# C in two buffers, GpSimd products two blocks wide, 28 weighed states, and the residual added by TensorE

## The chip, the cores and the metric

The kernel runs on one core of one Trainium2 chip. The metric is the device time of one execution in microseconds (us). The core has five engines that run their own instruction streams and meet only through semaphores: TensorE (PE in the profile, its weight loads PEld), VectorE (DVE), ScalarE (ACT), GpSimd (POOL) and SyncE (SP), which here only issues DMAs. SBUF is the on-chip memory, PSUM the memory that TensorE writes.

## The reference, cut to what matters

For 8 sequences of 1024 tokens, 512 features, the result is `x + mamba(layernorm(x)) + ffn(layernorm(x))`. The second term is the one that this change touches:

```python
xz = x @ W_in                       # 512 -> 2 * 1024
x_branch, z = split(xz)
xc = silu(causal_conv4(x_branch) + conv_b)
ssm = xc @ W_x                      # B (16), C (16) and one dt per token
dt = softplus(ssm[..., -1:] + dt_bias);  A = -exp(A_log)
for each token t:                   # h is [1024 channels, 16 states]
    h = h * exp(dt * A) + (dt * xc) * B
    y = sum over states of h * C
y = (y + xc * D_param) * silu(z)
out = x + y @ W_out + ffn
```

Everything is float32.

## The kernel before

The kernel has three phases. Phase W quantises the FFN's weights and phase A computes layer norm and FFN; it leaves `x + ffn` in the DRAM tensor `res_d`. Phase B computes the state-space term and adds it. Only phase B changes.

Phase B takes the 8192 tokens in 16 chunks of 512, two chunks to a sequence. The first chunk of a sequence (even) starts its scans at zero, the second (odd) at the states kept in `carry`. A chunk has 8 blocks of 128 channels, in two groups `g` of four, and 16 states. A slot `k` (0 to 31) is one state of one group; it has four steps, so that a step `n = 4k + j` runs from 0 to 127. In a step:

- ScalarE makes `decay = exp(dt * A)` (L1117) in one of three PSUM banks,
- GpSimd makes `v = u * B` (L963, function `drive`), with `u = dt * xc` and B of the state repeated over the partitions in `b_rep`; `v` has two buffers, one state each, and `v` of slot k may be written only when the scans of slot k-2 have read theirs,
- VectorE scans along the tokens, `hs = decay * hs + v` (L1159, `scan`), 128 channels by 512 tokens,
- TensorE turns one token tile of the previous state to tokens by channels (L1288, `ht`, two PSUM banks), and VectorE adds it to the sum, `acc = ht * C + acc` (L1173, `add_state`), C being one number per token from `c_now`.

For 20 of the 32 slots (the table `WEIGHED`) the last of the four token tiles takes another way: GpSimd multiplies the states by C (L971, `weigh`, output `hw`), TensorE turns and sums them in the PSUM bank `yw` (L1298), and VectorE adds that bank to `acc` once per group (L1181, `add_weighed`). So a chunk has 128 scans and 128 - 20 = 108 adds. GpSimd writes `hw` of slot k-2 right after the four `v` of slot k, and VectorE may not start the scans of slot k before `hw` of slot k-2 has been read out of the state buffer.

Between these steps stands the rest of the chunk's work, by tables of step or slot numbers: `MM` for TensorE (projections `ip` and `z`, convolution `cv`, `ssm`, turns `xd`, `yt`, and the output product `wo`, all through the two PSUM banks `mm`), `ACT_AT` for ScalarE (copies out of those banks, silu with its table loads, the parts of softplus), `POOL_AT` for GpSimd (`sp`: last add of softplus, `du`: `u = dt * xc`, `y2`: `acc * silu(z)`), `DVE_AT` for VectorE and `SP_AT` for SyncE. An engine waits at each such instruction for what it needs, and everything behind it on that engine waits too. ScalarE runs about two steps ahead of VectorE (three decay banks).

The output product `wo` of a token tile is four matmuls. After it VectorE adds the residual rows, `rtb = mm + rtb` (L1144), where SyncE has loaded `rtb` from `res_d` (`load`), and SyncE stores the sum (`store`). C of a chunk is copied by ScalarE from TensorE's bank to `c_next` (L1052) and by VectorE at step 4 to `c_now` (L1198), once the chunk before has used its own.

Of the kernel before, what the change touches and what calls it, by code (L numbers as in the profile page):

```python
# [16 lines left out]
ALU = mybir.AluOpType  # L17
ACT = mybir.ActivationFunctionType
# [618 lines left out]
def phase_b(nc, ctx, xnt, res, ssm_d, tap_d, ident, out, W_in, conv_w, conv_b, W_x, A_log, D_param, dt_bias, W_out):  # L637
# [27 lines left out]
    WEIGHED = (2, 3, 4, 6, 8, 10, 12, 13, 14, 15, 16, 17, 18, 19, 22, 23, 24, 25, 26, 30)  # L665
# [33 lines left out]
    c_now, c_next = sb("c_now", [P, NT, NS]), sb("c_next", [P, NT, NS])  # L699
# [17 lines left out]
    ct_done, ct_copied, c_set = sem("ct_done"), sem("ct_copied"), sem("c_set")  # L717
# [290 lines left out]
    def _(act):  # L1008
# [4 lines left out]
        def extra(c, what, *args):  # L1013
# [30 lines left out]
            if what in ("ssm", "ct"):  # L1044
# [86 lines left out]
    def _(dve):  # L1131
# [7 lines left out]
        def extra(c, what, g, t):  # L1139
            o = whose(c, what, g)  # L1140
            if o.exists(NC):
                wait(dve, rt_loaded[t % 2], o.at(64, 32 * g + 16 * (t // 2) + 16))
                wait(dve, wo_done, o.at(8, 4 * g + t + 1))
# [19 lines left out]
        def add_state(c, n):  # L1163

            g, s, k, t = n // 64, n // 4 % NS, n // 4, n % 4
            if s == 0 or (t == LT and all((NS * g + i, t) not in add_no for i in range(s))):
                wait(dve, acc_set, c.at(8, 4 * g + 4))
                if g == 0 and t == 0:
                    wait(dve, c_set, c.at(1, 1))
            else:  # L1170
# [3 lines left out]
                                           scalar=c_now[:, t, s:s + 1], in1=acc[g][:, t, :],  # L1174
# [9 lines left out]
        def part(c):  # L1184
            for n in range(4 * SLOTS):
# [174 lines left out]
```

## Time and profile before

| what | value |
|---|---|
| median of 3 runs | 5687.29 us (5685.86 to 5698.21) |
| the profiled execution | 5686.64 us, span 5684.8 us |
| busy share of the span | PE 86%, DVE 86%, POOL 70%, ACT 50% |
| phase B, first scan to last | 1935 to 5660 us |
| landing of one load of `rtb` | 4.2 us (median) |

Busy time is time in which an engine executes at least one instruction. One instruction's duration overlaps with the next one's by some tens of nanoseconds, so what an instruction costs its engine is read from start to start. The slices of the page before 1900 us are phases W and A, where TensorE is the busiest; from there on VectorE is at 9 tenths or more in each of them.

### The profile page before, as it was taken

The numbers are of one execution on the slowest core, as the hardware profiler recorded it, in microseconds if no ns is written. First come the engines' busy times: TensorE is split into PE (matmuls) and PEld (weight loads), VectorE is DVE, ScalarE is ACT, GpSimd is POOL, SyncE is SP. The second block draws the span as 40 slices with busy tenths as digits, with TensorE's granted clock in tenths as the row PEclk, the third lists the DMA queues.
The fourth block names the chain that finished last, engine by engine and source line by source line (L and its number), as shares of the span: only waits on it lengthen the run. The fifth ranks groups of instructions, "written<-read, shape, count | busy, mean of one in ns | idle before, by whom it ended". The sixth has DMA issues, their size and how long they took to land.

```text
span 5684.8 us, 79958 instructions
## 1 busy us (share of the span) xinstructions
PE 4886.1 (86%) x21764; PEld 3186.2 (56%) x21764; DVE 4871.6 (86%) x6055; ACT 2821.3 (50%) x4591; POOL 3984.9 (70%) x3130
## 2 busy tenths in 40 slices
PE   1799999999998788888888888888888888888867
PEld 1588888888886344444444444444444444444444
DVE  6676676676674399999999999999999999999998
ACT  1111111111111576666666666666667666667654
POOL 4333333333332499899999889989999998989996
PEclk9999999999999899999999999999999999999978
DMA  2111111111112222222232222322223232322221
GB/s 76 32 43 41 41 44 41 41 44 41 41 43 66 65 87 87 92 85 91 83 104 82 87 86 81 109 77 90 86 88 103 78 94 84 99 86 85 80 79 61
DMA packets 273645, 415.04 MB, mean 73 GB/s; under 512 B 31824, under 2 KB 105552, under 8 KB 269152
## 3 DMA queue, kind: packets, MB, share of 16 engines
q1 hardware_dynamic: 273248, 410.62, 22.8%
q8 instruction: 142, 2.33, 0.2%
q14 instruction: 255, 2.09, 0.1%
HBM read 340.23 MB, written 70.29 MB: 72 GB/s over the span
## 4 chain that ended last, share of the span: by engine, by line
DVE 23%; issue 18%; POOL 11%; PE 7%; ACT 7%; DVEq 1%; DMA 0%; POOLq 0%; ACTq 0%; SPq 0%
DVE hs L1159 14%; POOL v L963 8%; DVE acc L1173 8%; ACT decay L1117 3%; PE mm L1275 2%; PE ht L1288 2%; PE mm L1227 1%; DVEq L823 1%; POOL dt L989 1%; POOL sz L985 1%; ACT L1042 1%; POOL hw L971 1%; ACT xc L1042 1%; DVE rtb L1144 1%; PE mm L1244 1%
## 5 line engine op out<-in xcount | busy, mean ns | idle before, releaser
L963 POOL TENSOR_TENSOR v<-u,b_rep 128x512 f32<-128x512 f32 x2048 | 2555.2, 1274 | 201.9 <-DVE hs L1159 188.0
L1117 ACT ACTIVATE decay<-dt,a_neg 128x512 f32<-128x512 f32 x2048 | 1399.5, 688 | 1061.0 <-DVE hs L1159 1033.6
L1288 PEld LDWEIGHTS ht<-ident,hs 128*128 128x128 f32 x6912 | 827.8, 146 | 1503.4 <-issue 629.3
L1288 PE MATMUL ht<-ident,hs 128*128 128x128 f32 x6912 | 1127.5, 288 | 500.8 <-DVE acc L1173 318.6
L1159 DVE TENSOR_TENSOR_SCAN hs<-decay,v 128x512 f32<-128x512 f32 x1024 | 1232.3, 1216 | 152.3 <-POOL v L963 108.4
L1159 DVE TENSOR_TENSOR_SCAN hs<-decay,carry,v 128x512 f32<-128x512 f32 x1024 | 1293.3, 1275 | 26.7 <-ACT decay L1117 17.5
L1173 DVE SCALAR_TENSOR_TENSOR acc<-ht,c_now,acc 128x512 f32<-128x512 f32 x1728 | 1262.1, 730 | 11.9 <-PE ht L1288 11.4
L490 ACT ACTIVATE sg<-gate 128x512 f32<-128x512 f32 (+1 forms) x192 | 108.0, 563 | 1331.7 <-PE up L536 1331.7
L1275 PE MATMUL mm<-w_out,yt 128*128 128x512 f32 x1024 | 517.2, 612 | 43.5 <-ACT xb L1027 26.4
L1227 PE MATMUL mm<-x_in,w_in 128*128 128x512 f32 x1024 | 534.6, 634 | 21.3 <-DMA x_in<-xnt_d 17.8
L1244 PE MATMUL mm<-w_in,x_z 128*128 128x512 f32 x1024 | 507.0, 603 | 0.0
L1236 PE MATMUL mm<-xb,tap_diag 128*128 128x512 f32 (+3 forms) x1024 | 498.9, 599 | 2.7 <-ACT xc L1037 1.9
L106 POOL TENSOR_TENSOR h<-h,h_small 128x1408 f32<-128x1408 f32 x64 | 166.2, 2597 | 440.1 <-DVE h_small L100 440.1
L971 POOL TENSOR_TENSOR hw<-hs,c_rep 128x512 f32<-128x512 f32 x320 | 407.7, 1274 | 6.2 <-DVE hs L1159 6.2
L151 POOL TENSOR_TENSOR h<-h,h_small 128x1408 f32<-128x1408 f32 x64 | 166.3, 2598 | 333.7 <-DVE h L145 333.7
L435 DVE TENSOR_TENSOR rt<-down,rt 128x512 f32<-128x512 f32 x64 | 44.3, 692 | 322.2 <-PE down L536 322.2
L534 PE MATMUL gate<-gu,xqt 128*128 128x512 f32 (+1 forms) x768 | 300.7, 391 | 5.4 <-DVE xqt L426 5.4
L535 PE MATMUL gate<-gu,xqt 128*128 128x512 f32 (+1 forms) x768 | 288.8, 376 | 0.0
L536 PE MATMUL gate<-gu,xqt 128*128 128x512 f32 (+1 forms) x768 | 288.7, 376 | 0.0
L535 PE MATMUL up<-gu,xqt 128*128 128x512 f32 (+1 forms) x768 | 288.5, 376 | 0.0
L534 PE MATMUL up<-gu,xqt 128*128 128x512 f32 (+1 forms) x768 | 288.5, 376 | 0.0
L536 PE MATMUL up<-gu,xqt 128*128 128x512 f32 (+1 forms) x768 | 288.5, 376 | 0.0
(126 smaller groups left out, 7655.0 us busy)
## 6 DMA issues: line engine op xcount, KB each, us to landing
b_rep<-ssm_d SPq DMA_DIRECT2D x512, 256.0 KB, 3.4
tap_diag<-tap_d SPq DMA_DIRECT2D x128, 256.0 KB, 3.3
w_out<-in_L_attn_W_out SPq DMA_DIRECT2D x32, 1024.0 KB, 6.9
rtb<-res_d SPq DMA_DIRECT2D x128, 256.0 KB, 4.2
c_rep<-ssm_d SPq DMA_DIRECT2D x320, 64.0 KB, 3.2
xt<-in_L_attn_x SPq DMA_DIRECT2D x64, 256.0 KB, 2.8
xnt_d<-xntb SPq DMA_DIRECT2D x64, 256.0 KB, 2.7
rt<-in_L_attn_x SPq DMA_DIRECT2D x64, 256.0 KB, 2.6
```

The costliest lines, as they stand in the source:

```text
L534: nc.tensor.matmul(out, left_hi, right_hi, start=(k == 0), stop=False)
L535: nc.tensor.matmul(out, left_hi, right_lo, start=False, stop=False)
L536: last = nc.tensor.matmul(out, left_lo, right_hi, start=False, stop=(k == len(pairs) - 1))
L963: nc.gpsimd.tensor_tensor(v[k % 2][:, j, :], u[g][:, j, :], b_rep[k % 4][:, :], ALU.mult).then_inc(v_ready, 1)
L1117: nc.scalar.activation(decay[n % 3][:, :], dt[g][:, j, :], ACT.Exp, scale=a_neg[:, GD * g + j, s:s + 1]).then_inc(decay_ready, 1)
L1159: nc.vector.tensor_tensor_scan(h[k % 2][:, j, :], decay[n % 3][:, :], v[k % 2][:, j, :], carry[:, s, GD * g + j:GD * g + j + 1] if c.secon ...
L1173: nc.vector.scalar_tensor_tensor(out=acc[g][:, t, :], in0=ht[add_no[k, t] % 2][:, :, :].rearrange("p j d -> p (j d)"), scalar=c_now[:, t, ...
L1227: made, done = nc.tensor.matmul(bank[:, :], w_in[:, k, i * P:(i + 1) * P], x_in[:, k, :], start=first, stop=last), ip_done
L1236: made, done = nc.tensor.matmul(bank[:, skip:], tap_diag[i % 2][:, tap, :], xb[i % 2][:, tap + skip:tap + CL], start=first, stop=last), cv ...
L1244: made, done = nc.tensor.matmul(bank[:, :], x_z[:, k, t * P:(t + 1) * P], w_in[:, k, DI + g * GW:DI + (g + 1) * GW], start=first, stop=las ...
L1275: made, done = nc.tensor.matmul(bank[:, :], yt[t % 2][:, j, :], w_out[:, j, :], start=first, stop=last), wo_done
L1288: last = nc.tensor.transpose(ht[add_no[k, t] % 2][:, j, :], h[k % 2][:, j, t * P:(t + 1) * P], ident[:, :])
```

## The change

1. `c_now` becomes two buffers by chunk parity. ScalarE copies C straight into the one of its chunk, and VectorE's copy is gone, with `c_next` and the semaphore `c_set`.
2. `drive`, `sp`, `du` and `y2` work on two blocks per instruction (128 x 1024), B being repeated over the two by its access pattern. `POOL_AT` has 12 instructions in 12 entries where it had 24, and they stand at other slots: `y2` of group 1 at slots 3 and 4, `sp` and `du` at 7, 11, 29 and 31.
3. `WEIGHED` has 28 slots where it had 20: added are 0, 1, 7, 11, 20, 21, 28 and 31. Left out are 5, 9, 27 and 29.
4. `wo` has a fifth matmul, identity times the residual rows `rtb`, which waits for their load. ScalarE copies the bank into `rtb` (`add` in `ACT_AT`); `DVE_AT` is gone.
5. `ACT_AT` is written anew with these copies, 3 steps after the product's last matmul; silu of blocks 2 and 3 moves from step 38 to 47.

```diff
-    WEIGHED = (2, 3, 4, 6, 8, 10, 12, 13, 14, 15, 16, 17, 18, 19, 22, 23, 24, 25, 26, 30)
+    WEIGHED = (0, 1, 2, 3, 4, 6, 7, 8, 10, 11, 12, 13, 14, 15, 16, 17, 18, 19, 20, 21, 22, 23, 24, 25, 26, 28, 30, 31)
-    c_now, c_next = sb("c_now", [P, NT, NS]), sb("c_next", [P, NT, NS])
+    c_now = [sb(f"c_now{p}", [P, NT, NS]) for p in range(2)]
-    UNITS = {"ip": KH, "cv": KC, "z": KH, "wo": GD, "ssm": ND, "xd": 1, "yt": 1, "ct": 1}
+    UNITS = {"ip": KH, "cv": KC, "z": KH, "wo": GD + 1, "ssm": ND, "xd": 1, "yt": 1, "ct": 1}
...
             g = k // NS
-            for j in range(GD):
+            for j in range(0, GD, 2):
                 if j == 0:
                     wait(pool, b_loaded[k % 4], c.at(128, 16 * (k // 4) + 16))
                 if k % NS == 0:
-                    wait(pool, u_ready, c.at(8, 4 * g + j + 1))
-                wait(pool, scanned, c.at(128, 4 * (k - 2) + j + 1))
-                nc.gpsimd.tensor_tensor(v[k % 2][:, j, :], u[g][:, j, :], b_rep[k % 4][:, :], ALU.mult).then_inc(v_ready, 1)
+                    wait(pool, u_ready, c.at(8, 4 * g + j + 2))
+                wait(pool, scanned, c.at(128, 4 * (k - 2) + j + 2))
+                nc.gpsimd.tensor_tensor(v[k % 2][:, j:j + 2, :], u[g][:, j:j + 2, :],
+                                        b_rep[k % 4][:, :].unsqueeze(1).broadcast_to([P, 2, CL]),
+                                        ALU.mult).then_inc(v_ready, 2)
...
-                    wait(act, c_set, o.at(1, 0))
+                    wait(act, summed, o.at(ADDS, -ADDS))
                     wait(act, ct_done, o.at(1, 1))
-                    nc.scalar.activation(c_next[:, :, :], mm[bank_of("ct")][:, 0:NT * NS].rearrange("p (t s) -> p t s", t=NT),
+                    nc.scalar.activation(c_now[o.r % 2][:, :, :], mm[bank_of("ct")][:, 0:NT * NS].rearrange("p (t s) -> p t s", t=NT),
...
+            elif what == "add":
+                wait(act, wo_done, o.at(8, 4 * g + t + 1))
+                nc.scalar.activation(rt[t % 2][:, :], mm[bank_of("wo", g, t)][:, :], ACT.Copy).then_inc(added, 1)
...
-                nc.vector.tensor_tensor(rt[t % 2][:, :], mm[bank_of("wo", g, t)][:, :], rt[t % 2][:, :],
-                                        ALU.add).then_inc(added, 1)
...
-                if n == LAG - 1 and c.exists(NC):
-                    wait(dve, summed, c.at(ADDS, 0))
-                    wait(dve, ct_copied, c.at(1, 1))
-                    nc.vector.tensor_copy(c_now[:, :, :], c_next[:, :, :]).then_inc(c_set, 1)
...
-                made, done = nc.tensor.matmul(bank[:, :], yt[t % 2][:, j, :], w_out[:, j, :],
-                                              start=first, stop=last), wo_done
+                if last:
+                    wait(pe, rt_loaded[t % 2], o.at(64, 32 * g + 16 * (t // 2) + 16))
+                left, right = (ident[:, :], rt[t % 2][:, :]) if last else (yt[t % 2][:, j, :], w_out[:, j, :])
+                made, done = nc.tensor.matmul(bank[:, :], left, right, start=first, stop=last), wo_done
```

GpSimd, slots 1 to 5 of an odd chunk (v: products of one state, hw: weighed state, sz: `y2`). Before:

```order
L963 TENSOR_TENSOR v<-u,b_rep 128x512 x8
L985 TENSOR_TENSOR sz<-acc,sz 128x512 x2
L963 TENSOR_TENSOR v<-u,b_rep 128x512 x4
L985 TENSOR_TENSOR sz<-acc,sz 128x512 x2
L963 TENSOR_TENSOR v<-u,b_rep 128x512 x4
L971 TENSOR_TENSOR hw<-hs,c_rep 128x512
L963 TENSOR_TENSOR v<-u,b_rep 128x512 x4
```

Slots 3 to 5 of that chunk in the changed kernel:

```order
L960 TENSOR_TENSOR v<-u,b_rep 128x1024 x2
L970 TENSOR_TENSOR hw<-hs,c_rep 128x512
L985 TENSOR_TENSOR sz<-acc,sz 128x1024
L960 TENSOR_TENSOR v<-u,b_rep 128x1024 x2
L970 TENSOR_TENSOR hw<-hs,c_rep 128x512
L985 TENSOR_TENSOR sz<-acc,sz 128x1024
L960 TENSOR_TENSOR v<-u,b_rep 128x1024 x2
L970 TENSOR_TENSOR hw<-hs,c_rep 128x512
```

Each pair of narrow instructions is one wide one, a weighed product now stands in each of these slots, and one `y2` stands in each of two slots.

VectorE at the start of an odd chunk (hs: scan, acc: add), where the copy of C stood at step 4. Before:

```order
L1173 SCALAR_TENSOR_TENSOR acc<-ht,c_now,acc 128x512
L1159 SCALAR_TENSOR_TENSOR hs<-decay,carry,v 128x512
L1173 SCALAR_TENSOR_TENSOR acc<-ht,c_now,acc 128x512
L1198 COPY c_now<-c_next 128x64
L1159 SCALAR_TENSOR_TENSOR hs<-decay,carry,v 128x512
```

In the changed kernel, the first slots of that chunk:

```order
L1155 SCALAR_TENSOR_TENSOR hs<-decay,carry,v 128x512
L1169 SCALAR_TENSOR_TENSOR acc<-ht,c_now,acc 128x512
L1155 SCALAR_TENSOR_TENSOR hs<-decay,carry,v 128x512 x2
L1169 SCALAR_TENSOR_TENSOR acc<-ht,c_now,acc 128x512
L1155 SCALAR_TENSOR_TENSOR hs<-decay,carry,v 128x512
```

The copy is gone, and two scans stand together once per slot, where the fourth add was.

TensorE at the end of one output product of group 0 (mm: the shared banks). Before:

```order
L1275 MATMUL mm<-w_out,yt 128x512 x2
L1288 MATMUL ht<-ident,hs 128x128 x4
L1275 MATMUL mm<-w_out,yt 128x512
L1288 MATMUL ht<-ident,hs 128x128 x4
L1256 MATMUL mm<-ident,ssm_sb 128x16 x4
```

In the changed kernel:

```order
L1268 MATMUL mm<-w_out,yt 128x512 x2
L1280 MATMUL ht<-ident,hs 128x128 x4
L1290 MATMUL yw<-ident,hw 128x128 x4
L1268 MATMUL mm<-w_out,yt 128x512
L1280 MATMUL ht<-ident,hs 128x128 x4
L1268 MATMUL mm<-rtb,ident 128x512
L1246 MATMUL mm<-ident,ssm_sb 128x16 x4
```

The residual rows enter as a fifth product of the same size, one step later.

## Rows read from the trace of the kernel before

**Rows 1.** Windows of 233 us over phase B: time of the window, busy us (instructions) by engine.

```profile
sum 3726.00, PE 3143.45 PEld 1752.41 DVE 3622.32 ACT 2475.82 POOL 3388.55; mean PE 196.47 PEld 109.53 DVE 226.40 ACT 154.74 POOL 211.78
```

**Rows 2.** VectorE's groups in phase B: busy us, mean ns | idle before, releaser.

```profile
L1159 DVE TENSOR_TENSOR_SCAN hs<-decay,carry,v 128x512 f32<-128x512 f32 x1024 | 1293.3, 1275 | 26.7 <-ACT decay L1117 17.5 <-PE ht L1288 9.1
L1173 DVE SCALAR_TENSOR_TENSOR acc<-ht,c_now,acc 128x512 f32<-128x512 f32 x1728 | 1262.1, 730 | 11.9 <-PE ht L1288 11.4
L1159 DVE TENSOR_TENSOR_SCAN hs<-decay,v 128x512 f32<-128x512 f32 x1020 | 1227.4, 1216 | 45.4 <-ACT decay L1117 26.2 <-PE ht L1288 9.6 <-POOL hw L971 5.8
L1144 DVE TENSOR_TENSOR rtb<-mm,rtb 128x512 f32<-128x512 f32 x124 | 84.8, 684 | 17.0 <-PE mm L1275 16.8
L1198 DVE COPY c_now<-c_next 128x64 f32<-128x64 f32 x16 | 39.9, 2494 | 1.6
```

**Rows 3.** VectorE's waits in phase B: us in total, times, longest.

```profile
DVE hs L1159 <- ACT decay L1117: 43.7, 39, 1.8
DVE hs L1159 <- PE ht L1288: 18.7, 17, 1.6
DVE rtb L1144 <- PE mm L1275: 16.8, 19, 2.3
DVE hs L1159 <- POOL hw L971: 5.8, 4, 1.9
```

**Rows 4.** GpSimd's groups in phase B.

```profile
L963 POOL TENSOR_TENSOR v<-u,b_rep 128x512 f32<-128x512 f32 x2043 | 2549.1, 1274 | 201.9 <-DVE hs L1159 188.0 <-issue 12.6
L971 POOL TENSOR_TENSOR hw<-hs,c_rep 128x512 f32<-128x512 f32 x320 | 407.7, 1274 | 6.2 <-DVE hs L1159 6.2
L985 POOL TENSOR_TENSOR sz<-acc,sz 128x512 f32<-128x512 f32 x128 | 160.7, 1272 | 111.6 <-DVE acc L1173 41.9 <-DVE acc L1181 35.5 <-ACT sz L1059 34.1
L989 POOL TENSOR_TENSOR dt<-dt,u 128x512 f32<-128x512 f32 x124 | 157.9, 1273 | 0.0
```

**Rows 5.** Timeline of VectorE around one residual add: start, duration.

```profile
3507.89 0.73 DVE L1173 SCALAR_TENSOR_TENSOR acc<-ht,c_now,acc 128x512 f32<-128x512 f32 x1
3508.53 0.69 DVE L1144 TENSOR_TENSOR rtb<-mm,rtb 128x512 f32<-128x512 f32 x1
3509.13 2.33 DVE L1159 TENSOR_TENSOR_SCAN hs<-decay,v 128x512 f32<-128x512 f32 x2
3511.38 0.73 DVE L1173 SCALAR_TENSOR_TENSOR acc<-ht,c_now,acc 128x512 f32<-128x512 f32 x1
```

**Rows 6.** Timeline at two copies of C, the first with GpSimd at rest.

```profile
1941.50 0.17 DVE L1198 COPY c_now<-c_next 128x64 f32<-128x64 f32 x1
...
2867.29 1.27 POOL L985 TENSOR_TENSOR sz<-acc,sz 128x512 f32<-128x512 f32 x1
2867.48 2.37 DVE L1198 COPY c_now<-c_next 128x64 f32<-128x64 f32 x1
...
2869.76 1.21 DVE L1159 TENSOR_TENSOR_SCAN hs<-decay,v 128x512 f32<-128x512 f32 x1
```

**Rows 7.** GpSimd's groups by form, phase A: one operation at two widths.

```profile
L151 POOL TENSOR_TENSOR h<-h,h_small 128x1408 f32<-128x1408 f32 x64 | 166.3, 2598 | 333.7 <-DVE h L145 333.7
...
L151 POOL TENSOR_TENSOR xq<-xq,q_small 128x512 f32<-128x512 f32 x64 | 68.0, 1063 | 195.7 <-DVE xq L145 195.7
```

**Rows 8.** Timeline of GpSimd at slots 21 to 23 of an even chunk.

```profile
3004.37 3.82 POOL L963 TENSOR_TENSOR v<-u,b_rep 128x512 f32<-128x512 f32 x3
...
3014.25 2.50 POOL L985 TENSOR_TENSOR sz<-acc,sz 128x512 f32<-128x512 f32 x2 [4.29 <-ACT sz L1059]
3016.71 4.95 POOL L963 TENSOR_TENSOR v<-u,b_rep 128x512 f32<-128x512 f32 x4
```

**Rows 9.** The nearest forms to the new copy and the new product.

```profile
L1037 ACT ACTIVATE xc<-mm 128x512 f32<-128x512 f32 x128 | 75.2, 588 | 47.9 <-PE mm L1236 47.2
...
3001.87 1.88 PE L1244 MATMUL mm<-w_in,x_z 128*128 128x512 f32 x4
```

**Rows 10.** Timeline of the loads of residual rows behind a store.

```profile
3509.86 0.33 SPq L930 DMA_DIRECT2D rtb<-res_d  x1
...
3516.69 0.67 DVE L1144 TENSOR_TENSOR rtb<-mm,rtb 128x512 f32<-128x512 f32 x1
```

More of the change, by code:

```diff
@@ L771, in phase_b @@
-    DVE_AT = {21: [("add", 1, 0)], 29: [("add", 1, 1)], 42: [("add", 1, 2)], 50: [("add", 1, 3)],
-              94: [("add", 0, 0)], 99: [("add", 0, 1)], 104: [("add", 0, 2)], 109: [("add", 0, 3)]}
-    POOL_AT = {2: [("y2", 1, 0), ("y2", 1, 1)], 3: [("y2", 1, 2), ("y2", 1, 3)], 7: [("sp", 1, 0), ("du", 1, 0)],
[3 rows of a table removed]
+    ACT_AT = {4: [("silu_z", 1, 0), ("silu_z", 1, 1)], 6: [("ip", 0), ("abs", 1, 0)], 7: [("abs", 1, 1)],
+              8: [("abs", 1, 2)], 9: [("ip", 1), ("abs", 1, 3)], 10: [("exp", 1, 0)],
+              12: [("cv", 0), ("relu", 1, 0)], 13: [("yt", 1, 0), ("relu", 1, 1), ("exp", 1, 1)],
+              16: [("ip", 2), ("relu", 1, 2), ("relu", 1, 3)], 19: [("cv", 1)], 20: [("yt", 1, 1)],
+              21: [("ln", 1, 0), ("ln", 1, 1)], 23: [("add", 1, 0)], 26: [("ip", 3)], 28: [("xs", 1, 0)],
+              29: [("cv", 2)], 30: [("xs", 1, 1)], 31: [("silu_xc", 0), ("silu_xc", 1)], 33: [("add", 1, 1)],
+              34: [("yt", 1, 2)], 37: [("cv", 3)], 38: [("xd", 1, 0)], 39: [("xs", 1, 2)],
+              41: [("ip", 4), ("yt", 1, 3)], 42: [("xs", 1, 3)], 45: [("add", 1, 2)], 46: [("xd", 1, 1)],
+              47: [("silu_xc", 2), ("silu_xc", 3)], 49: [("ip", 5)], 53: [("xd", 1, 2), ("add", 1, 3)],
[3 rows of a table added]
+              87: [("z", 0, 3), ("silu_z", 0, 0), ("silu_z", 0, 1)], 92: [("ssm",), ("yt", 0, 0)],
+              93: [("yt", 0, 1)], 96: [("xs", 0, 0)], 97: [("abs", 0, 0), ("add", 0, 0)],
+              98: [("ct",), ("xs", 0, 1), ("abs", 0, 1)], 99: [("abs", 0, 2)], 100: [("abs", 0, 3)],
+              101: [("add", 0, 1)], 102: [("yt", 0, 2), ("exp", 0, 0)], 103: [("xd", 0, 0), ("exp", 0, 1)],
[4 rows of a table added]
@@ L973, in weigh, with extra @@
                                     ALU.mult).then_inc(weighed, 1)
-        def extra(c, what, g, j):
+        def extra(c, what, g, half):
             o = whose(c, what, g)
@@ L978, in extra @@
                 return
+            j = 2 * half
+            two = slice(j, j + 2)
             if what == "y2":
-                wait(pool, z_ready, o.at(4, 2 * g + j // 2 + 1))
-                if j == LT:
+                wait(pool, z_ready, o.at(4, 2 * g + half + 1))
+                wait(pool, summed, sums(o, NS * g + NS - 1, j + 1))
+                if half == LT // 2:
                     wait(pool, yw_added, o.at(2, g + 1))
-                else:
-                    wait(pool, summed, sums(o, NS * g + NS - 1, j))
-                nc.gpsimd.tensor_tensor(sz[:, j, :], acc[g][:, j, :], sz[:, j, :], ALU.mult).then_inc(y2_ready, 1)
+                nc.gpsimd.tensor_tensor(sz[:, two, :], acc[g][:, two, :], sz[:, two, :], ALU.mult).then_inc(y2_ready, 2)
             elif what == "sp":
-                wait(pool, sp_ops, o.at(16, 8 * g + 7 + j // 2))
-                wait(pool, relu_set, o.at(8, 4 * g + j + 1))
-                nc.gpsimd.tensor_tensor(dt[g][:, j, :], dt[g][:, j, :], u[g][:, j, :], ALU.add).then_inc(dt_ready, 1)
-            else:
-                wait(pool, xc_ready, o.at(ND, GD * g + j + 1))
-                wait(pool, dt_ready, o.at(8, 4 * g + j + 1))
-                nc.gpsimd.tensor_tensor(u[g][:, j, :], dt[g][:, j, :], xc[:, GD * g + j, :], ALU.mult).then_inc(u_ready, 1)
+                wait(pool, sp_ops, o.at(16, 8 * g + 7 + half))
+                wait(pool, relu_set, o.at(8, 4 * g + j + 2))
+                nc.gpsimd.tensor_tensor(dt[g][:, two, :], dt[g][:, two, :], u[g][:, two, :], ALU.add).then_inc(dt_ready, 2)
+            else:
+                wait(pool, xc_ready, o.at(ND, GD * g + j + 2))
+                wait(pool, dt_ready, o.at(8, 4 * g + j + 2))
+                nc.gpsimd.tensor_tensor(u[g][:, two, :], dt[g][:, two, :], xc[:, GD * g + j:GD * g + j + 2, :],
+                                        ALU.mult).then_inc(u_ready, 2)
         def part(c):
@@ L1137, in _ @@
             nc.vector.tensor_copy(w_x[:, :, a:a + n], w_x_raw[:, :, b:b + n]).then_inc(w_set, 1)
[L1139 to L1143, printed above, removed]
-                nc.vector.tensor_tensor(rt[t % 2][:, :], mm[bank_of("wo", g, t)][:, :], rt[t % 2][:, :],
-                                        ALU.add).then_inc(added, 1)
         def scan(c, n):
@@ L1168, in add_state @@
                 if g == 0 and t == 0:
-                    wait(dve, c_set, c.at(1, 1))
+                    wait(dve, ct_copied, c.at(1, 1))
             else:
@@ L1194, in part @@
                         add_weighed(owner, g)
-                if n == LAG - 1 and c.exists(NC):
-                    wait(dve, summed, c.at(ADDS, 0))
-                    wait(dve, ct_copied, c.at(1, 1))
-                    nc.vector.tensor_copy(c_now[:, :, :], c_next[:, :, :]).then_inc(c_set, 1)
-                for what in DVE_AT.get(n, ()):
-                    extra(c, *what)
         over_chunks(dve, part)
```

17 lines of the change are left out of this document (5 added, 12 removed), and 18 rows, old and new, of tables (ACT_AT, POOL_AT).

## The prediction

> **What bounds the kernel now.** I read the busy shares by stage first. Over phase B all engines stand in one row [rows 1]: of a window of 233 us VectorE is busy 226.4, GpSimd 211.8, TensorE 196.5, ScalarE 154.7. The 3726 us are 16 chunks of 232.9 us. VectorE's groups and waits come next [rows 2, 3]: it idles only 104 us in 3726, chiefly for decays (43.7), turned states (18.7), the output product (16.8) and weighed states (5.8). So VectorE's own work sets the time and its removal shortens the chunk one for one, until something else is late. GpSimd is the one to watch, 14.6 us a chunk behind. Its idle time is mostly waiting for VectorE [rows 4]: 188.0 us for scans that free `v`.
>
> What an instruction costs VectorE is its start-to-start time [rows 5]: an add 0.64 us (3507.89 to 3508.53), a residual add 0.60, a scan 1.125 (two in 2.25); in odd chunks the scan's mean is 0.059 us longer [rows 2], so 1.185. For GpSimd four `v` end 4.95 us after the first starts [rows 8], which with 1.274 for the last [rows 4] is (4.95 - 1.27) / 3 = 1.23 a step. Check: 128 `v`, 20 `hw` and 24 others make 172 x 1.23 = 211.6 us, as measured.
>
> **The change, VectorE's side.**
> - Eight more weighed slots remove 8 adds a chunk: 128 x 0.64 = 82 us. The add of `yw` stays, one a group.
> - The residual adds: 124 in phase B's windows x 0.60 = 74 us, and 17 us of waiting before them [rows 2] = 91 us.
> - The copy of C: 64 elements take 0.17 us with GpSimd at rest and 2.37 us beside it, ending only when the running GpSimd product has ended [rows 6]; the next scan starts 2.28 us after it started. 39.9 us in all, less 16 overlaps of 0.1: 38 us.
>
> The trace thus shows the copy held up for the length of GpSimd instructions. The Trainium skill (SBUF — State Buffer, "SBUF: two separate sides") calls the port pair of the two engines an exclusive lock held for the full instruction, for a VectorE operation in a 2-port mode or with two SBUF inputs. By it a copy left in place would now wait for instructions twice as long, some 38 us more; that is an estimate for a copy that is gone and so changes no sum.
>
> Together 82 + 91 + 38 = 211 us, 13.2 a chunk. VectorE's busy time falls from 226.4 to 226.4 - (211 - 17) / 16 = 214.3 us.
>
> A rule against moving the eight adds to GpSimd: the skill (Perfetto Trace Analysis, "Optimizing Scalar/DVE Operations") says that the two share an SBUF read port, so offloading between them might not help. Here the trace disagrees for these forms: 226.4 and 211.8 us busy in the same 233 [rows 1] must overlap by 205, with scans and adds at their usual step. Scans and adds read one operand from PSUM.
>
> **GpSimd's side.** A 128x1024 product doesn't stand in the trace. Bounds: twice a narrow one, 2.46 us a step; or less by the part that doesn't grow with width. Two widths of one operation give it [rows 7]: (2598 - 1063) / 896 = 1.713 ns an element, which leaves 1063 - 512 x 1.713 = 186 ns. Then a wide product lasts 2 x 1.274 - 0.186 = 2.36 us, a step of 2.32 after 0.045 of overlap. I take 2.32, since the form is the same but for what it reads; repeating an operand costs nothing in `hw`, which repeats C and takes the same 1274 ns [rows 4]. In a sentence that the sum does without: the skill (GPSIMD Engine Reference, "Elementwise — side-by-side cycle accounting") has 4497 ns for 2048 elements, and a line from there to 1274 at 512 estimates 2.35 at 1024.
>
> Per chunk: 64 + 12 = 76 wide x 2.32 = 176.3, 28 `hw` x 1.23 = 34.4, together 210.7. The 8 new `hw` (9.8) are paid by the 76 pairs (10.6). GpSimd is as busy as before in a chunk that VectorE could do in about 220: still second, but the room is small, and it is had only where the order allows.
>
> The order: `hw` of slot k-2 comes behind both `v` of slot k, and the scans of slot k wait for it. From the end of scans k-2, GpSimd needs 2.32 + 1.23 = 3.55 us, while VectorE has one slot, 4 x 1.125 + 3 x 0.64 = 6.42 us: 2.9 us of room. A slot costs GpSimd 5.87, so it gains 0.55 (0.79 in odd chunks) a slot. Where `sp` and `du` stand, two wide ones, 4.64 us go in at once; those slots (7, 11, 29, 31) have no `hw` due, so room is two slots: 2.32 + 4.64 + 4.64 + 1.23 = 12.83 against 12.84. One alone fits; the next ones come before it is made good. Walking even chunks so gives stalls of 1.1 at slot 0 (29 and 31 together), 1.5 at 5 (`y2` at 3 and 4), 1.2 at 8, 0.5 at 12, and 2.5 at 23 and 24, where the first `y2` still waits for silu (4.29 us) [rows 8] before `v` of 23 can follow: 6.8 us. Odd chunks, with 0.24 us more a slot, about 4. VectorE is idle anyway at some of these places (behind silu's table loads and at chunk starts), which takes about 2 off. I take 3.5 us a chunk, 56 in all; bounds 0 (all hidden) and 6.8 x 16 = 109.
>
> **The rest.** ScalarE gets 8 copies like that of `xc`, 0.59 each [rows 9], 4.7 us a chunk on an engine that has 78 free; they stand where decays are two steps ahead. TensorE gets 8 products; four take 1.88 us, 0.43 to 0.47 each [rows 9], 3.8 us a chunk beside 36 free. Their cover is the two `ht` banks. Cost 0; if a copy or product delays every fifth decay or turn, up to 0.5 each, 8 x 0.5 x 16 = 64 us. The new wait on TensorE is for the residual load, and all turns stand behind it. The tightest is tile 2 of group 0: loaded at 3509.86 behind the store, landing 4.2 us later at 3514.1, used at 3516.69 [rows 10]: 2.6 us spare, and the product uses it about as early as the add did. Cost 0 to 2 us a chunk; I take 0. SyncE's stores come when ScalarE's copy does, which runs ahead of VectorE, so its queue isn't later.
>
> Edges: before the first scan and behind the last one nothing is hidden. Wider pieces delay the first `v` and the first `y2` by about 1.1 us each (2.36 against 1.27), each waits for one more piece of input (1 to 2 us), and the last products add about 1: 6 us.
>
> **Sum.** 211 - 56 - 6 = 149 us less than the profiled execution's 5686.6 (0.7 under the median of the runs): 5537 us, a chunk of about 223.5.
>
> **The rivals.**
> - Nothing new is late: GpSimd's stalls all fall into idle time that exists. For it: its idle total stays above 8 us a chunk. Against: the walk above. 5686.6 - 211 + 6, about 5480.
> - GpSimd becomes the bound, the wide product saving nothing. 76 x 2.46 + 34.4 = 221.4, plus waits that no order removes, those for silu and the `yw` sum, (34.1 + 35.5) / 16 = 4.3 [rows 4], some of them shorter: 226.5 a chunk; (232.9 - 226.5) x 16 = 102, less 6: 5591. For it: the operation of rows 7 repeats one operand within its rows, which `v` does not. Against: the wider one there is cheaper per element, 1.85 against 2.08 ns.
> - The residual product holds TensorE's queue: 2 us a chunk behind the load, 32 us: 5569. Against: rows 10.
> - Slower than before: the wide product costs more than two narrow ones, and scans wait for it at every slot. It decides from (232.9 - 34.4 - 6) / 76 = 2.53 us a step; at 2.6 the chunk is 76 x 2.6 + 40.4 = 238, and the time 5686.6 + 5.1 x 16 + 6 = 5774. The port rule above, were it to hold for adds and scans, would end on this side too: no 82 us, and 128 more products of 1.23 in VectorE's way, 5537 + 82 + 157 = 5776. Rows 1 and 7 speak against both.
>
> **The numbers.** Forecast 0.61 (own range 5500 to 5575), nothing late 0.14, GpSimd bound 0.16, load late 0.04, slower 0.04, and 0.01 for gains and losses that cancel. The range 5475 to 5605 leaves out the slower case and the ends of the two beside it. A measurement of this kernel can tell 0.2%, 11 us, from no change: faster by more 0.95, within 0.01, slower 0.04.
>
> **What would show it.** Right: a wide product's mean near 2.36 us and steps of 2.32; adds 1600 instead of 1728; VectorE busy near 214 of each 223 us, with a new wait of scans for `hw` or `v`, some 50 us in all, chiefly at slots 0, 5, 8 and 23; GpSimd's waits for VectorE much under 188; no wait of TensorE for `rtb`'s load over some us. Wrong: a wide mean of 2.5 or more; scans waiting for decays or turns for over 100 us, which would mean that ScalarE or TensorE took the place; scans or adds longer than 1216, 1275 and 730 ns, which would mean that GpSimd's longer instructions hold VectorE's port.

## The result and the profile after

The changed kernel takes 5536.59 us (median of 4 runs, 5533.65 to 5541.77) against 5689.15 us for the kernel before in the same session: a ratio of 0.9731, 95% interval 0.9715 to 0.9746. The profiled execution went from 5686.6 to 5534.0 us, 152.6 less; forecast were 149 less and 5537.

The windows over phase B, as in [rows 1], now 16 of 223 us:

```profile
sum 3568.00, PE 3161.24 PEld 1798.30 DVE 3424.69 ACT 2516.29 POOL 3364.41; mean PE 197.58 PEld 112.39 DVE 214.04 ACT 157.27 POOL 210.28
```

VectorE and GpSimd stand where they were forecast (214.3 and 210.7 us a chunk). VectorE is still the busiest. Its groups, beside [rows 2] (busy us, mean ns | idle before, releaser):

```profile
L1155 DVE TENSOR_TENSOR_SCAN hs<-decay,carry,v 128x512 f32<-128x512 f32 x1024 | 1282.8, 1270 | 51.4 <-ACT decay L1121 38.3 <-POOL hw L970 10.0 <-issue 1.7
L1155 DVE TENSOR_TENSOR_SCAN hs<-decay,v 128x512 f32<-128x512 f32 x1019 | 1213.3, 1207 | 72.6 <-ACT decay L1121 38.0 <-POOL hw L970 14.4 <-POOL v L960 12.9
L1169 DVE SCALAR_TENSOR_TENSOR acc<-ht,c_now,acc 128x512 f32<-128x512 f32 x1600 | 1158.5, 724 | 12.8 <-PE ht L1280 11.7 <-issue 0.4
```

There are 1600 adds in place of 1728, and scans and adds last no longer than before, though twice as wide products run beside them. GpSimd's groups, beside [rows 4]:

```profile
L960 POOL TENSOR_TENSOR v<-u,b_rep 128x1024 f32<-128x1024 f32 x1024 | 2407.4, 2369 | 146.7 <-DVE hs L1155 142.7 <-POOL u L993 3.1 <-ACT u L1095 0.5
L970 POOL TENSOR_TENSOR hw<-hs,c_rep 128x512 f32<-128x512 f32 x448 | 574.3, 1282 | 10.4 <-DVE hs L1155 10.4
```

The wide product lasts 2369 ns (forecast 2.36 us). VectorE's waits, beside [rows 3] (us in total, times, longest):

```profile
DVE hs L1155 <- ACT decay L1121: 76.3, 50, 3.9
DVE hs L1155 <- POOL hw L970: 24.4, 27, 1.4
DVE hs L1155 <- POOL v L960: 12.9, 6, 3.0
DVE acc L1169 <- PE ht L1280: 11.7, 21, 0.9
DVE hs L1155 <- issue: 5.8, 5, 2.7
DVE hs L1155 <- PE ht L1280: 4.3, 3, 1.5
```

The largest row is the one for which the forecast had nothing: scans wait 76.3 us for decays, where it was 43.7. Counted by slot over the whole trace, slot 10 (steps 40 to 43) holds 48.2 us in 16 waits, one a chunk; before it held 22.4. The timeline there (start, duration; in brackets the idle time of the engine before, and what ended it):

```profile
2894.27 0.69 ACT L1121 ACTIVATE decay<-dt,a_neg 128x512 f32<-128x512 f32 x1
...
2899.14 1.02 PE L1268 MATMUL mm<-rtb,ident 128*128 128x512 f32 x2
...
2900.44 0.60 PE L1252 MATMUL mm<-ident,xs 128*128 128x128 f32 x4
...
2901.14 0.72 ACT L1074 ACTIVATE xs<-xc,dpar 128x512 f32<-128x512 f32 x1 [6.17 <-PE mm L1252]
2901.76 0.67 ACT L1121 ACTIVATE decay<-dt,a_neg 128x512 f32<-128x512 f32 x1
...
2902.54 1.22 DVE L1155 TENSOR_TENSOR_SCAN hs<-decay,v 128x512 f32<-128x512 f32 x1 [3.00 <-ACT decay L1121]
```

Read it backwards. The scan starts when the decay is made; the decay stands on ScalarE behind `xs`, ScalarE's product for the skip term, which had waited 6.17 us for the turn (`xd`) of the `xs` of block 1, whose buffer it writes. By the tables that turn now stands one TensorE step later, at 43 instead of 42, behind the fifth product `mm<-rtb`.

### The profile page after: what moved, and what is told of

Read it like the earlier page. It is cut to its first block, busy times and chain, and to the rows that moved or that the text cites. A ratio compares the mean times of both kernels' runs of the same rounds, so it can differ in the third digit from the quotient of the medians.

```text
span 5532.1 us, 79462 instructions
## 1 busy us (share of the span) xinstructions
PE 4907.6 (89%) x22020; PEld 3235.2 (58%) x22020; DVE 4671.0 (84%) x5783; ACT 2865.7 (52%) x4719; POOL 3961.5 (72%) x2042
## 3 DMA queue, kind: packets, MB, share of 16 engines
q1 hardware_dynamic: 291680, 419.02, 24.4%
## 4 chain that ended last, share of the span: by engine, by line
DVE 17%; issue 15%; PE 15%; POOL 9%; ACT 9%; DVEq 1%; DMA 0%; POOLq 0%; ACTq 0%; SPq 0%
DVE hs L1155 11%; DVE acc L1169 6%; POOL v L960 6%; PE mm L1217 4%; ACT decay L1121 4%; PE ht L1280 3%; PE mm L1268 3%; PE mm L1226 2%; POOL hw L970 2%; PE yw L1290 1%; DVEq L820 1%; POOL dt L989 1%; ACT L1130 1%; POOL sz L985 1%; PE mm L1234 1%
## 5 line engine op out<-in xcount | busy, mean ns | idle before, releaser
L960 POOL TENSOR_TENSOR v<-u,b_rep 128x1024 f32<-128x1024 f32 x1024 | 2407.4, 2369 | 146.7 <-DVE hs L1155 142.7
L1280 PEld LDWEIGHTS ht<-ident,hs 128*128 128x128 f32 x6400 | 782.5, 145 | 1189.8 <-issue 682.3
L1155 DVE TENSOR_TENSOR_SCAN hs<-decay,v 128x512 f32<-128x512 f32 x1024 | 1219.0, 1207 | 180.6 <-POOL v L960 121.0
L1280 PE MATMUL ht<-ident,hs 128*128 128x128 f32 x6400 | 1019.9, 284 | 306.8 <-DVE acc L1169 158.0
L1169 DVE SCALAR_TENSOR_TENSOR acc<-ht,c_now,acc 128x512 f32<-128x512 f32 x1600 | 1158.5, 724 | 12.8 <-PE ht L1280 11.7
L970 POOL TENSOR_TENSOR hw<-hs,c_rep 128x512 f32<-128x512 f32 x448 | 574.3, 1282 | 10.4 <-DVE hs L1155 10.4
L1217 PE MATMUL mm<-x_in,w_in 128*128 128x512 f32 x1024 | 539.7, 637 | 25.2 <-DMA x_in<-xnt_d 17.4
L1290 PE MATMUL yw<-ident,hw 128*128 128x128 f32 x1792 | 281.7, 282 | 49.8 <-DVE acc L1177 48.0
L534 PE MATMUL up<-gu,xqt 128*128 128x512 f32 (+1 forms) x768 | 288.6, 376 | 0.0
L535 PE MATMUL up<-gu,xqt 128*128 128x512 f32 (+1 forms) x768 | 288.5, 376 | 0.0
```

The costliest lines, as they stand in the source:

```text
L534: nc.tensor.matmul(out, left_hi, right_hi, start=(k == 0), stop=False)
L535: nc.tensor.matmul(out, left_hi, right_lo, start=False, stop=False)
L960: nc.gpsimd.tensor_tensor(v[k % 2][:, j:j + 2, :], u[g][:, j:j + 2, :], b_rep[k % 4][:, :].unsqueeze(1).broadcast_to([P, 2, CL]), ALU.mult ...
L970: nc.gpsimd.tensor_tensor(hw[w % 2][:, :, :], h[k % 2][:, :, LT * P:], c_rep[w % 4][:, :].unsqueeze(1).broadcast_to([P, GD, P]), ALU.mult) ...
L1155: nc.vector.tensor_tensor_scan(h[k % 2][:, j, :], decay[n % 3][:, :], v[k % 2][:, j, :], carry[:, s, GD * g + j:GD * g + j + 1] if c.secon ...
L1169: nc.vector.scalar_tensor_tensor(out=acc[g][:, t, :], in0=ht[add_no[k, t] % 2][:, :, :].rearrange("p j d -> p (j d)"), scalar=c_now[c.r % ...
```

## The experiments

The suspicion about slot 10 was tried first: only ScalarE's `xs` of block 3 is moved from step 42 to 46.

```diff
-  41: [("ip", 4), ("yt", 1, 3)], 42: [("xs", 1, 3)], 45: [("add", 1, 2)], 46: [("xd", 1, 1)],
+  41: [("ip", 4), ("yt", 1, 3)], 45: [("add", 1, 2)], 46: [("xd", 1, 1), ("xs", 1, 3)],
```

> The changed kernel with one entry of ScalarE's table moved: the fourth scaling of group 1 (xs) from step 42 to step 46. In the changed kernel it waits about 6.2 us a chunk for the turn xd of block 1, which the fifth matmuls have pushed from step 42 to 43 in TensorE's order, and decays queue behind it; VectorE waits 3.0 us a chunk at step 43. Theory A (ScalarE's queue is blocked by that wait): the 48 us at step 43 go, little comes back elsewhere; about 5495 (5485 to 5510), VectorE's waits for decays under 40 us. Theory B (the forecast's: the new waits are GpSimd's queue order, and step 43 only shows a chunk's slack being used): GpSimd takes the freed time, its waits at hw and v grow by what step 43 loses; 5525 to 5540.

Measured: 5484.34 us, ratio 0.9644 (0.9631 to 0.9657), 50 us less than the changed kernel (ratios 0.9644 and 0.9731, about ±12). The waits for decays, and those for `hw` below them:

```profile
DVE hs L1155 <- POOL hw L970: 27.6, 34, 1.4
DVE hs L1155 <- ACT decay L1121: 26.7, 33, 1.5
```

The wait at slot 10 is gone, and the waits for `hw` hardly grew (24.4 before the move). One place in ScalarE's order cost the changed kernel 50 us, 26 of which the change itself had added.

Next, GpSimd's products one block wide again, with the slots of before for `sp`, `du` and `y2`, everything else as changed:

```diff
-            for j in range(0, GD, 2):
+            for j in range(GD):
...
-                nc.gpsimd.tensor_tensor(v[k % 2][:, j:j + 2, :], u[g][:, j:j + 2, :],
+                nc.gpsimd.tensor_tensor(v[k % 2][:, j, :], u[g][:, j, :], b_rep[k % 4][:, :], ALU.mult).then_inc(v_ready, 1)
```

> The changed kernel with GpSimd's products one block wide again (v, softplus's last add, u and y2, and their slots as before), all else as changed: 28 weighed slots, residual on TensorE, two buffers of C. Forecast's theory: GpSimd has 180 narrow products a chunk, 180 x 1.23 = 221.4 us, plus waits of its own of about 4, so that it becomes the bound at 226 to 228 us a chunk: 5580 to 5620. Rival (width doesn't matter, since 221 is still under the 223 of the changed kernel, and narrow pieces free VectorE sooner): 5530 to 5550.

Measured: 5629.72 us, ratio 0.9894 (0.9879 to 0.9909), 93 more than the changed kernel and 10 above the top of the range expected. Its waits:

```profile
DVE hs L1152 <- POOL hw L969: 110.4, 40, 8.2
...
DVE hs L1152 <- POOL v L961: 30.0, 15, 3.8
```

and its phase B in one window, from 1946 to 5607 us:

```profile
sum 3661.00, PE 3186.75 PEld 1803.50 DVE 3427.05 ACT 2509.48 POOL 3531.50; mean PE 3186.75 PEld 1803.50 DVE 3427.05 ACT 2509.48 POOL 3531.50
```

GpSimd is busy 3531.5 of 3661 us, 96%, and scans wait 140 us for it. This is what the rival "GpSimd becomes the bound" looks like; the wide products, with their new slots, are what keeps the changed kernel out of it.

C in two buffers alone, on the kernel before:

```diff
-                    nc.vector.tensor_copy(c_now[:, :, :], c_next[:, :, :]).then_inc(c_set, 1)
```

> The kernel before with C in two buffers and VectorE's copy gone, nothing else. Forecast's term: 38 us less, 5649 (5645 to 5660). Rival: the copy's 2.4 us at step 4 covered decays that are late behind silu's table loads, so VectorE waits there instead and half or less comes, 5668 to 5687.

Measured: 5647.06 us, ratio 0.9926 (0.9911 to 0.9941): 42 us less, forecast 38.

The residual part alone, on the kernel before: the fifth product, ScalarE's copy and ScalarE's new table.

```diff
+                if last:
+                    wait(pe, rt_loaded[t % 2], o.at(64, 32 * g + 16 * (t // 2) + 16))
+                left, right = (ident[:, :], rt[t % 2][:, :]) if last else (yt[t % 2][:, j, :], w_out[:, j, :])
```

> The kernel before with the residual rows as fifth matmul and ScalarE's copy (and the new table of ScalarE), nothing else. Forecast's term: 91 us less, 5596. Theory A: the xs behind the turn that the fifth matmuls push back costs about 1.5 us more a chunk at step 43, so 91 - 25 = 66 less, 5621; the wait at step 43 shows here too, with only 20 weighed slots and narrow products. Rival: it doesn't show here, as it came with GpSimd's load: 5596.

Measured: 5664.04 us, ratio 0.9955 (0.9940 to 0.9970): 26 us less, under both theories' 66 and 91. Its waits show three losses:

```profile
DVE hs L1152 <- ACT decay L1118: 69.4, 39, 3.6
DVE acc L1166 <- PE ht L1281: 37.1, 38, 4.6
DVE hs L1152 <- POOL hw L969: 19.0, 11, 1.9
DVE hs L1152 <- PE ht L1281: 13.8, 14, 1.6
```

Decays cost 26 more than in [rows 3] (24 of it at slot 10, which holds 46.4 us), turned states 21 more (37.1 + 13.8 against 11.4 + 18.7), weighed states 13 more. With the copy of C, 0.29 us longer on the mean, that makes 64 of the 65 missing from 91 (72 by the two profiled executions). Of the turned states, 19.6 us are five waits at the start of an even chunk, where TensorE stands idle in the middle of a turn (`ht`). Neither theory has them; the last section comes back to this idle time.

The 28 weighed slots alone, on the kernel before:

```diff
-    WEIGHED = (2, 3, 4, 6, 8, 10, 12, 13, 14, 15, 16, 17, 18, 19, 22, 23, 24, 25, 26, 30)
+    WEIGHED = (0, 1, 2, 3, 4, 6, 7, 8, 10, 11, 12, 13, 14, 15, 16, 17, 18, 19, 20, 21, 22, 23, 24, 25, 26, 28, 30, 31)
```

> The kernel before with 28 weighed slots, nothing else: narrow products, residual on VectorE, copy kept. Forecast's term: 8 adds a chunk, 82 us less, if GpSimd had room; but GpSimd then has 221.4 us of narrow products in a chunk of 233 with its pieces of softplus at slots where hw is now due. With the waits that the narrow version of the changed kernel showed (VectorE 110 us for hw): 82 - 85, about 5685 (5660 to 5700), no faster. Rival (GpSimd's 221 us fit in 228): 5605 to 5625.

Measured: 5690.6 us, ratio 0.9995 (0.9985 to 1.0005): 128 adds fewer, and no gain. Two rows tell why: the copies of C but the first have a mean of 5317 ns where the kernel before has 2649, 15 x 2.67 = 40 us, and scans wait 32 us more for `hw`; the rest of the 82 goes in small waits (the profiled execution took 5700.8 us, 10 above the median, so these are a little high).

```profile
L1198 DVE COPY c_now<-c_next 128x64 f32<-128x64 f32 x15 | 79.8, 5317 | 0.0
```

```profile
DVE hs L1159 <- POOL hw L971: 37.5, 24, 3.0
```

The timeline of one copy:

```profile
3568.50 4.97 POOL L963 TENSOR_TENSOR v<-u,b_rep 128x512 f32<-128x512 f32 x4
...
3570.57 7.83 DVE L1198 COPY c_now<-c_next 128x64 f32<-128x64 f32 x1
...
3573.41 1.28 POOL L971 TENSOR_TENSOR hw<-hs,c_rep 128x512 f32<-128x512 f32 x1
...
3574.63 2.49 POOL L985 TENSOR_TENSOR sz<-acc,sz 128x512 f32<-128x512 f32 x2
...
3577.07 1.27 POOL L963 TENSOR_TENSOR v<-u,b_rep 128x512 f32<-128x512 f32 x1
3578.32 1.27 DVE L1159 TENSOR_TENSOR_SCAN hs<-decay,carry,v 128x512 f32<-128x512 f32 x1
...
3579.67 1.27 POOL L963 TENSOR_TENSOR v<-u,b_rep 128x512 f32<-128x512 f32 x1 [1.32 <-DVE hs L1159]
```

The copy of 64 elements is open for 7.83 us, through the ends of six products that follow each other without a gap, and ends at 3578.40, when the seventh has ended (3577.07 + 1.27 = 3578.34) and GpSimd itself waits, for a scan that stands behind the copy.

The changed kernel with the 20 weighed slots of before:

> The changed kernel with the 20 weighed slots of before, all else as changed. It leaves out the gain of 82 us of adds, and the load of 8 weighed products a chunk on GpSimd. Forecast: 5537 + 82 - 56 (the new GpSimd waits go) = 5563. By what the changed kernel's trace shows (VectorE waits 24 us for hw, 13 for v): 5537 + 82 - 25 = 5594 (5580 to 5610).

Measured: 5611.49 us, ratio 0.9863 (0.9848 to 0.9878), 75 more than the changed kernel and above both numbers, just outside the range. Waits for GpSimd are 24 us less than in the changed kernel (13.0 against 37.3), but those for turned states 28 more (44.2 against 16.0), chiefly here:

```profile
2839.27 0.47 PE L1280 MATMUL ht<-ident,hs 128*128 128x128 f32 x1 [5.38 <-issue]
...
2843.57 0.80 PE L1280 MATMUL ht<-ident,hs 128*128 128x128 f32 x3 [3.83 <-issue]
...
2844.40 0.75 DVE L1169 SCALAR_TENSOR_TENSOR acc<-ht,c_now,acc 128x512 f32<-128x512 f32 x1 [3.50 <-PE ht L1280]
```

One iteration of the kernel's loop is two chunks. Just after its jump TensorE stands 5.38 and 3.83 us, waiting for nothing that the profile shows, the second time after one of a turn's four pieces, and VectorE gets 3.50 of it. This comes after each of the five jumps, 17.4 us in all, so only some 58 of the 75 us belong to the adds and the waits for GpSimd.

To take away the waits for `hw`, GpSimd's weighed product was put between the two pairs of `v` of its slot, in the kernel with the moved `xs`:

```diff
+                drive(c, k, (0,))
...
+                if c.exists(NC):
+                    drive(c, k, (2,))
```

> The changed kernel with xs later (as in the first experiment, 5484) and GpSimd's weighed product of slot k-2 ahead of the second pair of v of slot k instead of behind it; both wait for the same scans. Theory (order in GpSimd's queue makes the waits for hw): the room of hw grows from 2.9 to 5.2 us, VectorE's 28 us of waiting for hw fall under 8, those for v stay: 5462 (5455 to 5472). Rival (GpSimd is short of throughput at those slots, so the wait only changes its name): waits for v take over, 5480 to 5488.

Measured: 5467.48 us, ratio 0.9606 (0.9593 to 0.9619), less than the kernel it was built on by 17 (medians) or 22 (ratios), as expected. The theory of the order holds: of VectorE's waits in phase B none is for `hw`, and those for `v` rose from 3.6 to 9.0 us only. Those for turned states rose from 12.5 to 29.1 us, which no run explains.

```profile
DVE hs L1157 <- ACT decay L1123: 29.9, 40, 1.5
DVE acc L1171 <- PE ht L1282: 24.5, 22, 2.8
DVE hs L1157 <- POOL v L960: 9.0, 3, 3.3
```

On top of that, silu of `z` one at a time, at steps 3, 7, 83 and 87 (and the copy of the last `z` at step 84 instead of 87):

> As the one before, and the two silu of z, that stand together behind one table load at steps 4 and 87, each on its own with its own table load (steps 3 and 7, 83 and 87). Theory: a burst of 4.6 us on ScalarE outlasts the decays that VectorE has in hand, a burst of 3.6 does not: waits at steps 5 and 88, (5.2 + 21.2 us) together, fall to a few: 5440 (5432 to 5450) if the one before gives 5462. Rival: four more table loads a chunk (5.1 us on ScalarE) delay copies, gain under 10 us.

Measured: 5455.3 us, ratio 0.9586 (0.9573 to 0.9599), 11 ± 10 less than the kernel before it; expected were 27, or under 10 by the rival, from which the 11 can't be told. The waits at slots 1 and 22 went, but a new one of 1.2 us a chunk came at step 8.

GpSimd's wide products and their table alone, on the kernel before:

> The kernel before with GpSimd's v, softplus's last add, u and y2 two blocks wide (and their new slots), nothing else. VectorE bounds that kernel and 10.6 us a chunk fewer on GpSimd lie off its path: forecast's theory 5690, within 10 us of before. Rival from the weighed-only run, where VectorE's copy of C ended only when GpSimd's queue ran dry (up to 8.2 us): with more gaps on GpSimd the copy ends sooner and the kernel gains 10 to 20 us; or, if wide pieces run back to back at step 4, it takes longer and the kernel loses as much. The copy's mean tells which (2.49 us before).

Measured: 5666.93 us, ratio 0.9957 (0.9942 to 0.9973): 24 us less, and the row shows where they come from.

```profile
L1201 DVE COPY c_now<-c_next 128x64 f32<-128x64 f32 x15 | 2.9, 196 | 1.6
```

The copy falls from 2649 to 196 ns, 15 x 2.45 = 37 us, more than the whole gain: `y2` no longer stands beside it, and in 15 of the 16 chunks it runs while GpSimd stands idle.

The changed kernel with VectorE's copy of C kept:

```diff
+                    nc.vector.tensor_copy(c_now[:, :, :], c_next[:, :, :]).then_inc(c_set, 1)
```

> The changed kernel with VectorE's copy of C and the single buffer kept, all else as changed. Theory of the forecast (a copy waits for the one product that runs, now twice as long): mean about 3.6 to 5 us, 5537 + 60 to 80 = 5600 to 5617. Theory from the weighed-only run (it waits until GpSimd has nothing ready to run): GpSimd has no gap in slots 0 to 4 of a chunk, and VectorE is what its next products wait for, so the copy lasts 7 us or more in most chunks: 5537 + 110 = 5650 (5630 to 5700). If neither holds and the copy lasts 0.2 us: 5540.

Measured: 5541.12 us, ratio 0.9734 (0.9719 to 0.9749): 2 us more, ± 12. Neither forecast number comes; the third, 5540, comes without its 0.2 us copy.

```profile
L1194 DVE COPY c_now<-c_next 128x64 f32<-128x64 f32 x15 | 15.8, 1051 | 0.0
```

One of these copies:

```profile
3282.77 2.36 POOL L960 TENSOR_TENSOR v<-u,b_rep 128x1024 f32<-128x1024 f32 x1 [0.35 <-DVE hs L1155]
...
3284.32 0.87 DVE L1194 COPY c_now<-c_next 128x64 f32<-128x64 f32 x1
3285.08 1.27 POOL L970 TENSOR_TENSOR hw<-hs,c_rep 128x512 f32<-128x512 f32 x1
```

It ends at 3285.19, with the product that ran when it started (3285.13), though the next one follows without a gap. So do 15 of this kernel's 16 copies, which is what the first theory says; its number fell because the copies start late in a product and not at its beginning.

The changed kernel with the residual rows on VectorE again and the tables of before for ScalarE and VectorE:

```diff
+                nc.vector.tensor_tensor(rt[t % 2][:, :], mm[bank_of("wo", g, t)][:, :], rt[t % 2][:, :],
+                                        ALU.add).then_inc(added, 1)
```

> The changed kernel with the residual rows added by VectorE as before (four matmuls, VectorE's table and ScalarE's table of before), all else as changed. Forecast's term: 91 us more, 5628. Theory A (the fifth matmuls cost about 25 us at step 43 behind xs): 66 more, 5603, with 1.4 us a chunk of waiting at step 43 instead of 3.0. The residual alone, on the kernel before, gave 26.

Measured: 5607.93 us, ratio 0.9853 (0.9838 to 0.9868), 69 more than the changed kernel: the theory that charges the part with the wait at slot 10, where scans now wait 25.1 us.

Last, the kernel with the split silu and two of softplus's steps earlier:

```diff
-    ACT_AT = {3: [("silu_z", 1, 0)], 6: [("ip", 0), ("abs", 1, 0)], 7: [("silu_z", 1, 1), ("abs", 1, 1)],
+    ACT_AT = {3: [("silu_z", 1, 0)], 5: [("abs", 1, 0)], 6: [("ip", 0), ("abs", 1, 1)], 7: [("silu_z", 1, 1)],
```

> The split-silu version (5455) with two softplus pieces (abs of blocks 0 and 1) one step earlier on ScalarE, so that none stands with the burst at step 7. Theory (VectorE's 19 us of waiting at step 8 are the burst plus the piece beside it): 5440 (5432 to 5450). Rival (another queue takes it): 5450 to 5460.

Measured: 5448.47 us (5445.56 to 5453.37), ratio 0.9574 (0.9561 to 0.9587). Against the split silu alone the interval takes in no change, and the wait at step 8 is still there (17.1 us of 19.2), so the theory of the piece beside the burst isn't borne out. Against the changed kernel it is (0.9731 - 0.9574) x 5690 = 89 us less: the lowest time of all, together with the split silu alone from which it can't be told, and faster than both kernels. Its waits in phase B:

```profile
DVE hs L1157 <- ACT decay L1123: 22.0, 34, 1.6
DVE acc L1171 <- PE ht L1282: 11.9, 17, 2.0
DVE hs L1157 <- issue: 8.2, 4, 2.7
DVE hs L1157 <- POOL v L960: 7.1, 2, 3.6
```

## Why the prediction was right, and where it wasn't

The sum of the prediction beside what the two traces show, in us:

| term | forecast | measured | from |
|---|---|---|---|
| VectorE's work that goes | -194 | -197.6 | busy in the two windows rows, 3622.3 and 3424.7 |
| its waits for the output product | -17 | -16.8 | [rows 3], gone after |
| waits for GpSimd | +56 | +29.9 | 24.4 + 12.9, before 5.8 + 1.6 |
| waits for decays | 0 | +32.6 | 76.3 - 43.7 |
| waits for turned states | 0 | -14.1 | 16.0 - 30.1 |
| "issue" | 0 | +4.0 | 6.2 - 2.2 |
| before the first scan and from the last one on | +6 | +9.3 | first scan 4.65 later; last one to the end 30.7 against 26.0 |
| sum | -149 | -152.7 | |

**What held.** VectorE bounds the kernel, and what leaves it leaves the time; the width law from two widths of another operation gave 2.36 us for the product (2369 ns, two in 4.70 us, a step of 2.33); new waits for GpSimd came at slots 0, 8 and 24, as walked; no wait of TensorE for the residual load shows; scans and adds did not grow. One sign came only in part: GpSimd's waits for scans fell from 188.0 to 142.7 us, which is not much under.

**The step that failed** is that of "The rest": ScalarE and TensorE "Cost 0". The fifth product moves the turn `xd` by a step, and ScalarE's next `xs` waits for that turn with the decays queued behind it. I had asked whether the new copies delay decays, and not which instruction of ScalarE waits for one that the new product pushes back. Of the 33 us by which waits for decays grew, 26 are at that place, slot 10, where the kernel before already had 22 of its 43.7. The first experiment shows that this `xs` holds them; the residual part is what adds them, since slot 10 has 46.4 us with that part alone and 25.1 with it left out. These two runs change the fifth product and ScalarE's table together; that the product does it and not the table is read from the timeline, where the turn ends last. The other 7 us are mostly at slot 1 (8.0 us, before 1.3), where VectorE's copy of C stood; that the copy had covered them was not tested by itself.

TensorE's own cost was mis-read as well. The row behind "four take 1.88 us" counts records of the trace, and each matmul of this form leaves two:

```profile
L1268 PE MATMUL mm<-rtb,ident 128*128 128x512 f32 x250 | 127.9, 593 | 0.0
```

These are 125 products of 1.02 us, 8.2 us a chunk where the sum had 3.8. No run shows what that doubling costs by itself.

**Another term mis-sized.** GpSimd's stalls came out at 30, not 56. By slot, waits for `hw` or `v` over 0.3 us are at slot 0 (8.1 for `hw` and, without the first scan of all, 11.7 us for `v`), 8 (7.6) and 24 (7.0); at 5 and 23, where the walk had 1.5 and most of 2.5 us a chunk, there are none. The walk started each one with no room in hand. The two errors, 26 too much and 33 too little, nearly cancel: the time fitted better than its parts, and the 14 of turned states helped.

**The parts don't add.** Alone they give 42, 26, 3 and 24 us, 95 together; the whole gives 153. Left out one at a time they are worth 2 (copy), 69 (residual), 75 (weighed) and 93 (width). Two of these numbers hold TensorE's idle time inside a turn, which neither the kernel before nor the changed one has: without it the residual part alone would be worth some 46, and the weighed slots left out some 58 (estimates from the 19.6 and 17.4 us above). The runs show two couplings. The copy's price hangs on GpSimd's order: 42 us to be had before, 2 after, since beside the moved and wide products it lasts 1.05 us and not 2.65. And the eight weighed slots, worth nothing alone, lose 40 of their 82 us to longer copies and 32 to waits for `hw` there; in the changed kernel the copy is gone and the wide products make room. Which of the two they need more, no run separates. My 38 for the copy was thus right for the kernel before. It isn't wrong in the sum either, as the copy's 39.9 us are gone from VectorE whichever part takes them.

**The copy's mechanism.** I wrote that it ends when the running GpSimd product has ended. My own [rows 6] say otherwise: that product ends at 2868.56 and the copy at 2869.85. Nor is GpSimd at rest at their first copy, the one of 0.17 us at 1941.50:

```profile
1937.85 7.42 POOL L963 TENSOR_TENSOR v<-u,b_rep 128x512 f32<-128x512 f32 x6
```

The third of these six products ends at about 1941.6, so this copy fell on the seam between two of them. With GpSimd truly idle the copy takes 0.20 us (15 copies with the wide products alone, mean 196 ns). The sum hardly changes: it took the copies' total, 39.9 us.

In the five traced kernels that keep the copy, 34 of 80 copies outlast the running product, by up to six more (7.83 us above), and every one of these ends only when GpSimd then stands idle for 1.26 us or more, mostly because it waits for a scan behind the copy. The others end with the running product, or run while there is none. The Trainium skill (SBUF — State Buffer, "SBUF: two separate sides") has the loser of the shared port blocked for the whole of the other's instruction; the copy of 7.83 us outlasts that by six instructions, so the rule is too weak here, though 15 of 16 copies fit it in the kernel with the copy kept. The 38 us more that I estimated from it for a copy left in place don't come: that kernel's copies are 15.8 us, the kernel before's 39.9. Why a waiting copy is let in at the first end in one place and only at a gap in another stays open.

## What to carry to other kernels

When an instruction is added to an engine's queue, look past its own time: list what it pushes back there, and which engine waits for each of these with critical work behind it. A part's worth read from the kernel before is its worth alone; where two parts touch the same engine pair, price each with the other in place. Before using a row's count, find out how many records one instruction leaves. When a total fits, compare the terms all the same: here one mis-placed instruction hid 50 us.

## What the hardware showed beyond that

- A VectorE copy from SBUF to SBUF, 0.20 us with GpSimd at rest (wide products alone), took up to 8.22 us beside back-to-back GpSimd products (in the kernel with the weighed slots alone), while scans and adds, which read one operand from PSUM, don't lengthen: 1207 and 724 ns in the changed kernel, with GpSimd busy 94% of phase B, and 1216 and 730 before.
- TensorE stood idle for 4.6 to 6.6 us after each of the loop's five jumps, in all 14 traces, put down to "issue". In two kernels, the residual part alone and the 20 weighed slots, a second idle time of 3.6 to 4.8 us falls inside the turn that follows, and VectorE waits 3.0 to 4.6 us each time. The kernel before has the same TensorE order there as the one with the residual part alone, and no second one. What causes either was not found.
